# The one-hot matrices of an on-chip inversion, made by five wide bfloat16 comparisons in place of 33 narrow ones

## The reference

```python
y = einsum('bct,bcd->bdt', x, cond_w[itok])            # 32 sequences, 32 channels
probs = softmax(y @ w_router); top_w, top_i = top_k(probs, 4)   # 16 experts
g = silu(y @ we1[e]) * (y @ we3[e]) * cw               # H = 128, chosen experts
moe = g @ we2[e]
shared = silu(y @ ws1) * (y @ ws3) @ ws2               # HS = 512
out = x + shared / 5 + moe * 4 / 5
```

## Time and profile before

| | |
|---|---|
| median of 3 runs | 145.71 us (145.31 to 148.47) |
| profiled execution, own time | 145.43 us |
| its span, first to last instruction | 143.7 us |
| PE busy | 132.7 us, 92% |
| DVE busy | 102.7 us, 71% |
| ACT busy | 71.3 us, 50% |
| POOL busy | 65.8 us, 46% |
| mean granted clock of PE | 0.992 |

### The profile page before, as it was taken

One profiled execution on the slowest core, in us unless ns is written; L12 is line 12 of the kernel. 1 busy time (PEld: TensorE's weight loads), 2 busy tenths in 40 slices (PEclk: granted clock), 3 DMA queues, 4 the chain that ended last, 5 costly groups with the idle time before them and its releaser, 6 DMA issues.

```text
span 143.7 us, 2783 instructions
## 1 busy us (share of the span) xinstructions
PE 132.7 (92%) x800; PEld 110.8 (77%) x800; DVE 102.7 (71%) x271; ACT 71.3 (50%) x164; POOL 65.8 (46%) x79
## 2 busy tenths in 40 slices
PE   5987988988989999999999999999999999999770
PEld 2337677767758699999799999999999978888550
DVE  1301799999669997786998899767677562167992
ACT  4002799999456534535435544486435231108900
POOL 0600000002777877776656785776586777000000
PEclk9999999999999999999999999999999999999996
DMA  1923889989955756678777574544442122399924
GB/s 34 299 56 85 217 280 274 378 269 299 362 182 164 203 177 206 196 237 292 215 233 207 198 282 166 187 183 183 160 173 112 73 110 114 79 393 414 389 78 146
DMA packets 23742, 29.82 MB, mean 208 GB/s; under 512 B 4112, under 2 KB 20496, under 8 KB 23600
## 3 DMA queue, kind: packets, MB, share of 16 engines
q1 hardware_dynamic: 19632, 19.86, 41.4%
q0 software_dynamic: 3120, 8.52, 18.1%
q10 hardware_dynamic: 976, 1.26, 2.7%
HBM read 17.58 MB, written 6.42 MB: 167 GB/s over the span
## 4 chain that ended last, share of the span: by engine, by line
PE 57%; DVE 17%; DMA 13%; POOL 5%; issue 4%; DVEq 1%; ACT 0%; ACTq 0%; SPq 0%; POOLq 0%
PE up_ps L1027 18%; PE down_ps L1043 13%; PE gate_ps L980 5%; POOL store_t L452 5%; PE up_ps L923 4%; PE gate_ps L923 4%; PE down_ps L936 4%; DVE store_t L716 4%; PE down_ps L1005 3%; PE up_ps L1021 2%; DMA raw<-in_L_ffn_we 2%; DMA itok_rows<-in_itok_B 2%; DMA store_t<-y_of,token_i 2%; DMA g<-in_L_cond_weights,cond_idx 2%; DMA xt<-store_t 2%
## 5 line engine op out<-in xcount | busy, mean ns | idle before, releaser
L452 POOL DMA_INDIRECT store_t<-y_of,token_i x32 | 31.5, 984 | 39.3 <-DVE token_i L725 27.2
L459 POOL DMA_INDIRECT result<-store_t,back_i x32 | 31.3, 980 | 12.9 <-DVE store_t L807 7.1
L807 DVE SCALAR_TENSOR_TENSOR store_t<-down_ps,valid,store_t 128x256 f32 x47 | 21.5, 458 | 8.4 <-DVE store_t L807 5.1
L1043 PE MATMUL down_ps<-w,gt 128*128 x94 | 24.4, 381 | 0.0
L1027 PE MATMUL up_ps<-w_hi,x_hi 128*128 x78 | 23.6, 303 | 0.3 <-DVE x_lo L773 0.3
L1027 PE MATMUL up_ps<-w_lo,x_hi 128*128 x78 | 21.9, 281 | 0.0
L1027 PE MATMUL up_ps<-w_hi,x_lo 128*128 x78 | 21.9, 281 | 0.0
L564 ACT ACTIVATE gt<-down_ps 128x256 f32<-128x256 f32 (+1 forms) x24 | 9.1, 380 | 21.0 <-PE down_ps L1005 19.9
L1043 PEld LDWEIGHTS down_ps<-w,gt 128*128 128x128 f32 x94 | 16.2, 190 | 1.9 <-issue 0.5
L572 ACT ACTIVATE sil<-up_ps 128x256 f32<-128x256 f32 (+1 forms) x24 | 9.1, 380 | 15.6 <-PE up_ps L1027 11.6
L1027 PEld LDWEIGHTS up_ps<-w_hi,x_hi 128*128 128x128 f32 x78 | 14.8, 189 | 0.6 <-issue 0.6
(11 more groups left out here) (158 smaller groups left out, 235.1 us busy)
## 6 DMA issues: line engine op xcount, KB each, us to landing
xt<-store_t SPq DMA_DIRECT2D x43, 128.0 KB
raw<-in_L_ffn_we SPq DMA_DIRECT2D x30, 128.0 KB, 3.4
w<-in_L_ffn_we SPq DMA_DIRECT2D x4, 512.0 KB, 6.3
w_lo<-result SPq DMA_DIRECT2D x4, 512.0 KB, 6.6
raw<-result SPq DMA_DIRECT2D x4, 512.0 KB, 6.5
acc<-in_x SPq DMA_DIRECT2D x2, 512.0 KB, 4.6
y_of<-store_t ACTq DMA_DIRECT2D x1, 1024.0 KB, 5.2
out<-acc SPq DMA_DIRECT2D x3, 256.0 KB, 2.2
```

What stands on the lines that cost most here:

```text
L452: pool.indirect_dma_start(xs[:, j, :], None, y_of, bass.IndirectOffsetOnAxis(ap=token_i[:, j:j + 1], axis=0),).then_inc(tile_in[j % TT], 16)
L459: pool.indirect_dma_start(result, bass.IndirectOffsetOnAxis(ap=back_i[:, j:j + 1], axis=0), merged[:, j, :], None,).then_inc(result_out[j ...
L807: dve.scalar_tensor_tensor(out=into, in0=out_ps[n % 2][:, h, :], scalar=valid[:, it:it + 1], in1=into, op0=ALU.mult, op1=ALU.add).then_inc ...
L1043: last = pe.matmul(out_ps[b][:, h, :], gt[:, b, h, :], w2_of(experts[2 + h]), start=True, stop=True)
```

## The change

- `row_hot` and `tile_hot` are laid out with the number of the choice innermost: `row_hot` as (c, r, n) with 8 choices n, `tile_hot` as (j, n) with 32 choices n.
- At the start, two copies write the counts out in full (`row_count`, each of 0 to 127 eight times; `tile_count`, each of 0 to 31 thirty-two times), into tiles of `store_t` that are free then. They take the place of `count_r`.
- After L682, two copies turn the tile and the row numbers into bfloat16 (`tile_b`, `row_b`) ahead of the comparison of tiles. They take the place of `row_f`, which came behind it.
- One comparison of two bfloat16 tensors makes `tile_hot`, and one for each `c` makes eight of the matrices of `row_hot`.
- The readers step: ACT reads `tile_hot` with its innermost index 32 elements (64 bytes) apart, and PE loads each matrix of `row_hot` with its columns 8 elements (16 bytes) apart.

```diff
-        row_hot = early(16, 8).bitcast(BF16).rearrange("p (n r) -> p n r", r=P)
-        tile_hot = early(24, 2).bitcast(BF16).rearrange("p (n j) -> p n j", j=TILES)
+        row_hot = early(16, 8).bitcast(BF16).rearrange("p (c r n) -> p c r n", c=TOP_K, r=P)
+        tile_hot = early(24, 2).bitcast(BF16).rearrange("p (j n) -> p j n", j=TILES)
...
-        count_r = small[:, 640:640 + P // 2].bitcast(BF16)
+        counts = store_t[:, TT:TT + 4, :].rearrange("p t d -> p (t d)").bitcast(BF16)
+        row_count = counts[:, 0:P * TT].rearrange("p (r n) -> p r n", n=TT)
+        tile_count = counts[:, P * TT:P * TT + TILES * TK].rearrange("p (j n) -> p j n", n=TK)
...
-                    act.activation(dest_hot[:, :, 0, :], tile_hot, ACT.Copy, scale=part[:, 0:1]).then_inc(dest_hot_done, 1)
-                    hot = tile_hot.rearrange("p (t k) j -> p t k j", k=TOP_K)
+                    act.activation(dest_hot[:, :, 0, :], tile_hot.rearrange("p j n -> p n j"), ACT.Copy, scale=part[:, 0:1]).then_inc(dest_hot_done, 1)
+                    hot = tile_hot.rearrange("p j (t k) -> p t k j", k=TOP_K)
...
-            step(dve.tensor_copy(count_r[:, :], count_w))
+            step(dve.tensor_copy(row_count, spread(count_w, TT)))
+            step(dve.tensor_copy(tile_count, spread(count_i[:, :], TK)))
...
-            dve.tensor_tensor(tile_hot, repeat(count_i[:, 0:TILES], TK), spread(tile_i[:, :], TILES), ALU.is_equal).then_inc(tile_hot_done, 1)
-            chain(dve.tensor_copy(row_f[:, :], row_i[:, :]))
+            step(dve.tensor_copy(tile_b, tile_i[:, :]))
+            chain(dve.tensor_copy(row_b, row_i[:, :]))
+            dve.tensor_tensor(tile_hot, repeat(tile_b, TILES), tile_count, ALU.is_equal).then_inc(tile_hot_done, 1)
...
             def rows_hot(c):
-                for n in range(TT * c, TT * c + TT):
-                    dve.tensor_scalar(row_hot[:, n, :], count_r[:, :], row_f[:, n:n + 1], None, ALU.is_equal).then_inc(row_hot_done, 1)
+                dve.tensor_tensor(row_hot[:, c, :, :], repeat(row_b[:, TT * c:TT * c + TT], P), row_count, ALU.is_equal).then_inc(row_hot_done, 1)
...
-                        pe.wait_ge(row_hot_done, n + TT)
-                    last = pe.matmul(dest_ps.rearrange("p m j -> p (m j)"), row_hot[:, n, :], dest_hot[:, n, :, :].rearrange("p m j -> p (m j)"),
+                        pe.wait_ge(row_hot_done, n // TT + 1)
+                    last = pe.matmul(dest_ps.rearrange("p m j -> p (m j)"), row_hot[:, n // TT, :, n % TT], dest_hot[:, n, :, :].rearrange("p m j -> p (m j)"),
```

More of the change, by code:

```diff
@@ L159, in adaln_ffn @@
         ones = small[:, 576:576 + P // 2].bitcast(BF16)
-        count_r = small[:, 640:640 + P // 2].bitcast(BF16)
+        counts = store_t[:, TT:TT + 4, :].rearrange("p t d -> p (t d)").bitcast(BF16)
+        row_count = counts[:, 0:P * TT].rearrange("p (r n) -> p r n", n=TT)
+        tile_count = counts[:, P * TT:P * TT + TILES * TK].rearrange("p (j n) -> p j n", n=TK)
         later = early(8, 2)
         tile_i, row_i = (later[:, k * TK:(k + 1) * TK].bitcast(I32) for k in range(2))
-        row_f, token_f = (later[:, k * TK:(k + 1) * TK] for k in range(2, 4))
+        token_f = later[:, 3 * TK:4 * TK]
+        row_b, tile_b = (later[:, 2 * TK:3 * TK].bitcast(BF16)[:, k * TK:(k + 1) * TK] for k in range(2))
         parts = later[:, 128:128 + 4 * E].rearrange("p (m e) -> p m e", e=E)
```

## The result

The changed kernel takes 149.89 us (median of 4, 148.99 to 150.17), the kernel before 145.67 us beside it. These medians lie 4.2 us apart. The ratio, taken over the fast runs of each kernel alone, is 1.0254, 95% interval 1.0206 to 1.0303: slower by 3.7 us, or 2.5%. The forecast was 147.8, the range 145.0 to 149.7. The median lies 0.2 us above the upper end; by the ratio, from the 145.43 us that the forecast started from, the time is 149.1, inside the range. The profiled execution took 149.83 us with a span of 148.1.

The account below looks back on a forecast made before the run. Bound: nearly equal DVE and ACT chains ahead of L724, then gathers and the full PE pair stage. ACT's stepped reading adds 2.5 us, L724 moves +2.4, so 145.43 + 2.4 = 147.8 us; range 145.0 to 149.7.

Parts of the forecast that it names:

- What bounds the kernel, and what DVE's saving is worth: Before L724: DVE's comparisons end last, ACT's chain only 0.13 us earlier, so saving 0.6 to 2.8 us gains 0.1 us.
- the cover: ACT is busy until 27.04, hiding when tile_hot is ready (26.45, or 26.97 unpaired), so the faster tile comparison gains nothing.
- The cost of the comparisons and of the counts: On DVE: 0.71 us per 1024-element comparison if paired; count copies at most 1.22 us each at the start, costing nothing.
- ACT's reading: ACT's 13 copies reading 3,072 elements 64 bytes apart: time per element doubles, 0.82 ns more each, 2.5 us more.
- a choice between two ends: For ACT's 64-byte steps: from nothing to fourfold, 7.6 us more; the double, 2.5 us, was taken.
- PE's weights: PE's weight loads in 16-byte steps for the inversion: no change taken, 0.042 us a load; doubled would add 1.3 us.
- the lower end: For PE's weight loads in 16-byte steps: no change, as for 8-byte steps.
- L907's spacing: Sign at PE's inversion matmuls: 0.043 or 0.08 us between them would tell whether the stepped weights cost time.
- rival 3: ACT's reading and PE's weight loads both double: PE multiplies from 33.55 to 36.4, +3.1, 148.5 us; chance 0.16.
- `dest_hot` is ready at 33.5. PE, idle from 30.9, multiplies until 35.15.: At the inversion: ACT's copies end 2.5 us later, PE's 32 matrices take 1.6 us, L724 starts at 35.75, +2.4.
- rival 4: ACT's element costs three steps or more: 5.0 us, 150.3 us; idle PE possibly losing clock counted here; chance 0.18.
- All shift by about as much and keep their places.: Work behind ACT's copies and PE's wait (high parts, silu(2), silu(3), first shared half) shifts by about the same 2.4 us.

Follow-up runs that it names:

- rows_only: The changed kernel with its tile part undone (tile_hot made and read as before) and the wide row comparisons kept; ratio 0.9985 to the kernel before.
- steps_measured: The kernel before with short operations added near its start, reading in various steps on ACT, DVE and PE, for the trace alone; 150.19 us, one run.
- tiles_only: The changed kernel with its row part undone (32 narrow comparisons, weights as neighbours) and the tile part kept; ratio 1.0259 to the kernel before.
- pe_busy: The changed kernel with 14 extra matmuls of 512 columns, result overwritten, ahead of the inversion's matmuls; ratio 1.0179 to the kernel before.
- pe_reads_steps: The changed kernel with dest_hot also laid out choice innermost, PE reading its 96 columns in 64-byte steps; ratio 1.0349 to the kernel before.
- pe_half_busy: The changed kernel with 7 extra matmuls of 512 columns ahead of the inversion's matmuls; ratio 1.0157 to the kernel before.

## Why the prediction was partly right

- *What bounds the kernel, and what DVE's saving is worth.* Right. rows_only has DVE done 2.7 us earlier (29.99 against 32.72) and measures no difference; the 0.1 us of the sum can't be told from nothing. `tile_hot` was ready at 26.91 in the changed kernel, ahead of ACT's 27.49, as the cover wanted it.
- *The cost of the comparisons and of the counts.* Right: 0.69 us against 0.71, and the first products were not delayed by the counts (one copy of 1024 took 0.69 us, against my bound of 1.22).
- *ACT's reading.* Right in kind, and 2.7 us against 2.5; steps_measured has 0.9 ns more an element against my 0.82. The size was a choice between two ends, and that it came out is partly luck. The rule of the Trainium skill, "SBUF — State Buffer" (the note on cachelines in "Door 1: The DMA port swizzle"), asks for two accesses to each 16-byte line. For reading it agrees: 8 bytes free, 16 and more not, in either type. The same note has 4 float32 or 8 bfloat16 elements as the free step, which is 16 bytes; if that is meant to hold 16 itself, it differs from 0.64 us against 0.40, and the measurement decides. L650, the row that spoke against a cost, said nothing of this memory. The Trainium skill, "Vector Engine (DVE) Microarchitecture Reference", section 5.2, gives 0.68 ns more for one hopping source; DVE's 256 elements here cost 0.16 us more at 64 bytes, 0.63 ns each.
- *PE's weights.* I took the lower end and it was between: 0.06 us a load instead of 0.043. I had read L898's 0.042 us as the pace of the loads; steps_measured has 0.03 with neighbours, so the load did double, from a lower base. And the sign that I had named for it, L907's spacing, misleads: the changed kernel shows 0.08 us, rival 3's figure, but tiles_only shows it with neighbours, so it is the clock.
- *"`dest_hot` is ready at 33.5. PE, idle from 30.9, multiplies until 35.15."* This is the step that failed. `dest_hot` was ready at 33.7 (net), but the matrices took 2.78 us and not 1.6, since PE had lost its clock in the pause, and L728 came 3.2 us late and not 2.4. I had named that, but only inside rival 4 and without a price or a chance of its own. With the clock held (pe_busy) L728 is 2.7 us late. There the ratios give 2.3 to 2.6 us for the whole kernel, but that this is the forecast's 2.4 is in part luck: the two profiled executions, 148.79 and 148.92, lie 3.4 to 3.5 above the 145.43 that the forecast started from.
- *"All shift by about as much and keep their places."* Failed too. The wide matmuls behind the inversion ran at the lower level, seven at 0.2 us more, `gated(3)` came 4.7 us late and not 2.7, and DVE's low parts became what ends last. The delay at the pair stage was 4.3 us. Not all of this growth is the clock's: with the clock held it was 3.9, behind a gather that landed in 4.29 us, as one did in rows_only without any delay of the inversion.
- *Sum.* Forecast 2.4; measured 3.7 by the ratio, 4.2 by the medians. ACT's reading makes the most of it, 2.3 to 2.6; the clock has a part of 0.2 to 1.1, and the late start of 0.45 us, seen in both traces of the changed kernel, may be the rest.

What stays open: how much the clock costs, and how it splits between the inversion and what follows; why the first load landed late in both traces of the changed kernel; and why the gathers landed in 3.05 us in one trace and 4.3 in others. In tiles_only the clock came back 3 us earlier than in the changed kernel (36.8 against 39.9) at the same total. Against that gain stands, in its trace, the pause of 1.38 us in the pair stage; what made it is open, too.

## What to carry to other kernels

A layout that makes one engine's operation wide must be priced at every reader: here 2.8 us of a waiting engine's time were bought with 2.7 us of the engine on the path. Look in the timeline for the engine whose work begins when the shortened one ends, and ask whether it was ready earlier; if not, the saving is worth nothing until work is moved over to the engine that has been freed. And when an edit makes a pause for PE in a stage where it is otherwise full, write down a price for the lower clock behind the pause.

## What the runs showed of the hardware

- Reading SBUF in steps: ACT pays nothing at 8 bytes and 0.9 ns more an element from 16 to 64 bytes, in bfloat16 and float32 alike (steps_measured).
- Writing 2-byte elements apart is dearer: 4.7 ns an element at 192 bytes (1024 in 4.83 us against 1.04 by neighbours); four copies of 256 at 8 bytes took 2.48 us against 1.32, while runs of four 2-byte elements cost next to nothing (1.73 against 1.69).
- PE: bfloat16 weights every 0.03 us at 4 and 8 bytes, 0.06 at 16; 96 columns to multiply in steps of 64 bytes 0.17 us a matrix against 0.043, at either level of the clock.
- The granted clock held at 1.00 over a pause of PE of 1.62 us, and fell to half in or behind pauses of 2.16, 2.73, 3.10 and 3.21 us. In pe_reads_steps it fell behind a pause of only 1.58 us, over 3 us after PE had begun to work again. It came back after some 3 to 6 us of work, not always after the same.
- The landing of one and the same gather took 3.05 us in the trace of before and 4.3 in those of rows_only, pe_busy and pe_half_busy.
